# Identity of the self loops: from PSUM on ScalarE to SBUF on GpSimd, with another DRAM layout of two matrices

## The chip, the cores and the metric

The kernel runs on one NeuronCore of one Trainium2 chip. The time is the device time of one launch, in microseconds; the median of three runs of the kernel before is 2294.6 us (2289.54 to 2294.87). Engines are named as in the profile: PE is TensorE, PEld its weight load, DVE VectorE, ACT ScalarE, POOL GpSimd, SP the engine that issues most DMAs.

## The reference

A chain of four residual blocks over 3125 nodes with 256 features and 100000 edges. Edges come sorted by destination, and low destinations have many more edges than high ones (the square of a uniform number).

```python
dst = jnp.minimum((3125 * jax.random.uniform(..., (100000,)) ** 2.0).astype(jnp.int32), 49999)
...
def _spmm(src, dst, w, x, n):                       # used twice, with edge weights
    return jax.ops.segment_sum(w[:, None] * x[src], dst, num_segments=n)
for W, b, g, be in ((W1, b1, g1, be1), (W2, b2, g2, be2)):
    agg = _spmm(src, dst, edge_weight, x, n)
    h = (x + agg) @ W + b                           # the x here is the self loop
    x = jax.nn.gelu(_layer_norm(h, g, be), approximate=False)
...
def gcn_conv(x, edge_index, W, b, n_nodes):         # used twice, with counts
    loops = jnp.arange(n_nodes, dtype=edge_index.dtype)
    ...                                             # loops are joined to src and dst
    deg = jax.ops.segment_sum(jnp.ones_like(dst, dtype=x.dtype), dst, num_segments=n_nodes)
    dinv = jnp.where(deg > 0, jax.lax.rsqrt(deg), 0.0)
    ...
x = x + L0_gnn(layernorm(x)); x = x + L0_ffn(layernorm(x)[None])[0]
x = x + L1_gnn(layernorm(x)); x = x + L1_ffn(layernorm(x)[None])[0]
```

## The kernel before, in words

The sums over edges are done as dense products. The kernel first builds two matrices of 3200 x 3200 float32 (padded nodes): the weight matrix (the sum of edge weights between two nodes, plus the identity) and the count matrix (the number of edges, plus the identity). Both go to DRAM. Three passes then read them back in pieces and multiply them with the features.

**The build** takes the destinations in 400 windows of 8 nodes. Edges stand in chunks of 128; each meeting of a chunk with a window is a *pair*, 1200 with the padding at the end. Three engines work on pairs at once.

- DVE makes one-hot matrices for a batch of 8 pairs (six instructions, lines 993 to 998; 150 batches). Three batches may lie ahead of PE.
- PE adds each pair into PSUM with four bf16 matmuls (three at line 1353 for the weight's three parts, one at line 1354 for the counts). Two windows are a *group* and have two banks; the eight banks hold four groups. PE waits on `acc_free` before it writes into a group's banks, and each pair adds to `pair_done`.
- ACT takes a finished group (wait on `pair_done`): line 579 copies the two banks to `stage[half]` in SBUF, line 585 zeroes them, a drain follows, and line 553 (`self_loops`) writes the two windows' piece of the identity into both matrices' accumulators, which frees the banks (`acc_free`). PE then adds to it.

Ten groups (160 nodes) are a *unit*, and there are 20 units. `stage` has two halves, used in turn. At a unit's end ACT raises `unit_complete` right after the last copy, and copies the degree row (line 557, `degrees_of`, adds to `unit_summed`). SP waits for `unit_complete` and issues the two writes of the unit at line 474, 2 MB each, to the weight and to the count matrix. Before ACT fills a half again, `stage_free` waits until both writes of that half's last unit have landed and its degrees are taken; then ACT loads the unit's ten limits from a table (line 570). At the end ACT, PE and DVE meet in `compute_end`.

Eight matmuls at line 1330 write all banks once ahead of the build (`banks_opened`), and ACT waits for them.

**The passes** read a block of 320 columns (two units) in five DMAs of 800 KB (line 507; the first block at line 477) into `ring`, and PE multiplies (line 1417, `stream`), 1500 products of 128x128 by 320 float32 columns, with the layers' other work beside them. `ring` and `stage[0]` share memory, so the first block's DMAs wait until the second last unit is written.

There is a second way through the build for edges that are not sorted (`disordered > 0`); these inputs do not take it.

## Time and profile before

| | us |
|---|---|
| median of three runs | 2294.6 |
| the profiled run's own time | 2289.54 |
| its span in the trace | 2287.8 |
| build, first pair on PE to ACT's last copy of degrees | 107.6 to 692.8 |
| first product of the passes | 699.1 |

| engine | busy us | share of the span |
|---|---|---|
| PE | 2064.8 | 90% |
| DVE | 957.0 | 42% |
| ACT | 623.0 | 27% |
| POOL | 49.6 | 2% |

The shares are means over stages with different limits: in the passes PE is busy all the time, in the build it is not. The profile page says, for each group of instructions, how long it ran, and how long its engine was idle just before and what ended that. The granted clock of TensorE is given as a share of full speed (1.0 is 2.4 GHz, 0.5 is 1.2 GHz).

### The profile page before, as it was taken

To read this page: it belongs to the slowest core of one execution; us is meant where nothing else is said; L and a number is where in the kernel's file an instruction comes from. 1 tells how busy PE (TensorE), PEld (TensorE's weight loads), DVE (VectorE), ACT (ScalarE), POOL (GpSimd) and SP (SyncE) were. 2 spreads that over 40 slices of the span, in tenths; PEclk is the share of its full clock that TensorE was granted. 3 is DMA by queue.
4 is the path that set the end of the run, shared out by engine and by line. 5 is a ranking of instruction groups with operands and counts; after the bars stand their busy time and mean duration, and the time that the engine had idled before them with its cause. 6 is when DMAs were issued, how large, how long until landed. Compare 5 with 4: busy or idle time off the path is not lost.

```text
span 2287.8 us, 32669 instructions
## 1 busy us (share of the span) xinstructions
PE 2064.8 (90%) x11143; PEld 1596.8 (70%) x11144; DVE 957.0 (42%) x1977; ACT 623.0 (27%) x1057; POOL 49.6 (2%) x58
## 2 busy tenths in 40 slices
PE   1698888887678999999999979999999989999997
PEld 1388788777666777777777756657777767777776
DVE  5899999987760111111233332221332232222222
ACT  0014577787781200000111023320000012212121
POOL 2000000000000000000000000000000000000000
PEclk7799999998988999999999989989999999999999
DMA  2001333433457444444433310004334420000000
GB/s 77 1 0 72 143 143 143 197 161 161 198 213 216 127 136 140 142 143 137 125 115 126 115 58 1 0 0 144 115 117 127 128 89 1 12 12 0 11 11 10
DMA packets 70915, 221.13 MB, mean 97 GB/s; under 512 B 10300, under 2 KB 27354, under 8 KB 65754
## 3 DMA queue, kind: packets, MB, share of 16 engines
q1 hardware_dynamic: 56554, 213.41, 27.0%
q10 hardware_dynamic: 14320, 7.18, 1.3%
q8 instruction: 26, 0.43, 0.1%
q14 instruction: 15, 0.12, 0.0%
HBM read 135.45 MB, written 85.12 MB: 96 GB/s over the span
## 4 chain that ended last, share of the span: by engine, by line
issue 54%; PE 30%; DVE 8%; ACT 4%; ACTq 2%; DVEq 1%; DMA 0%; SPq 0%; POOL 0%; POOLq 0%
PE ps L1353 8%; PE ps L1434 8%; PE ps L1586 8%; DVE act_c L998 4%; PE ps L1354 3%; ACT ps L585 2%; ACT wide L579 2%; ACTq L570 1%; PE ps L1417 1%; PE ps L1325 1%; DVE act_c L993 1%; PE ps L1610 1%; DVE wide L1287 0%; DMA wide<-in_edge_weight_dram 0%; PE ps L1466 0%
## 5 line engine op out<-in xcount | busy, mean ns | idle before, releaser
L1353 PE MATMUL ps<-early,act_c 128*128 128x200 bf16 x3600 | 473.2, 261 | 105.4 <-ACT ps L553 47.7
L1417 PE MATMUL ps<-wide 128*128 128x320 f32 x2000 | 547.0, 434 | 0.0
L1417 PEld LDWEIGHTS ps<-wide 128*128 128x128 f32 x2000 | 379.3, 191 | 154.4 <-issue 1.7
L1353 PEld LDWEIGHTS ps<-early,act_c 128*128 128x128 bf16 x3600 | 343.0, 101 | 138.7 <-issue 131.4
L1354 PE MATMUL ps<-early,act_c 128*128 128x208 bf16 x1200 | 316.6, 264 | 0.0
L998 DVE TENSOR_TENSOR act_c<-act_c,pair_tab 128x1024 bf16<-128x1024 bf16 x450 | 282.9, 682 | 0.0
L1417 PE MATMUL ps<-wide,act_a 128*128 128x320 f32 x1000 | 274.7, 437 | 8.8 <-ACTq L618 8.8
L1417 PEld LDWEIGHTS ps<-wide,act_a 128*128 128x128 f32 x1000 | 192.1, 193 | 88.8 <-issue 11.8
L579 ACT COPY wide<-ps 128x816 f32<-128x816 f32 x200 | 167.2, 836 | 177.7 <-PE ps L1354 134.8
L1287 DVE SCALAR_TENSOR_TENSOR wide<-ps,small,wide 128x256 f32<-128x256 f32 x200 | 82.0, 477 | 266.6 <-PE ps L1434 266.4
L1095 DVE TENSOR_TENSOR wide<-ps,rows 128x1280 f32<-128x1280 f32 x10 | 14.9, 1492 | 419.4 <-PE ps L1434 419.4
L1586 PE MATMUL ps<-act_a,wide 128*128 (+1 forms) x640 | 188.9, 451 | 0.0
L1434 PE MATMUL ps<-early,act_c 128*128 128x256 f32 x800 | 181.8, 383 | 2.3 <-DVEq L1289 2.3
L1434 PEld LDWEIGHTS ps<-early,act_c 128*128 128x128 f32 x800 | 153.7, 192 | 28.0 <-issue 2.7
L585 ACT ACTIVATE ps<-ones 128x816 f32<-128x816 f32 x200 | 170.6, 853 | 8.1
L771 ACT ACTIVATE act_c<-ps,cols 128x320 f32<-128x320 f32 x160 | 84.4, 527 | 322.4 <-PE ps L1586 322.4
L1586 PEld LDWEIGHTS ps<-act_a,wide 128*128 128x128 f32 x640 | 125.5, 198 | 54.3 <-issue 11.0
L994 DVE TENSOR_TENSOR early<-rows 128x1600 bf16<-128x1600 bf16 x150 | 147.3, 982 | 0.0
L993 DVE TENSOR_TENSOR act_c<-rows,pair_tab 128x1024 bf16<-128x1024 bf16 x150 | 102.5, 684 | 70.3 <-PE ps L1354 68.8
L1354 PEld LDWEIGHTS ps<-early,act_c 128*128 128x128 bf16 x1200 | 121.3, 101 | 2.3
L692 ACT COPY wide<-ps 128x1280 f32<-128x1280 f32 x10 | 12.3, 1226 | 323.6 <-PE ps L1440 323.6
L717 ACT ACTIVATE act_c<-ps,cols 128x320 f32<-128x320 f32 x90 | 46.1, 524 | 101.4 <-PE ps L1508 99.3
(197 smaller groups left out, 1305.9 us busy)
## 6 DMA issues: line engine op xcount, KB each, us to landing
wide<-weight_matrix SPq DMA_DIRECT2D x100, 800.0 KB, 4.5
weight_matrix<-wide SPq DMA_DIRECT2D x20, 2000.0 KB, 6.2
count_matrix<-wide SPq DMA_DIRECT2D x20, 2000.0 KB, 10.8
wide<-count_matrix SPq DMA_DIRECT2D x50, 800.0 KB, 4.5
x_nodes<-in_x_dram ACTq DMA_DIRECT2D x1, 3072.0 KB
out_dram<-x_nodes SPq DMA_DIRECT2D x4, 640.0 KB
early<-in_L_ffn_w_dram SPq DMA_DIRECT2D x8, 256.0 KB, 5.4
wide<-in_L_ffn_w_dram SPq DMA_DIRECT2D x8, 256.0 KB, 4.2
```

The source lines that it names most:

```text
L579: act.copy(stage[half][:, :, k * GCOLS:(k + 1) * GCOLS].rearrange("p r (b j) -> p b r j", b=GROUP), group_ps.rearrange("p b (r j) -> p b r ...
L585: act.activation(group_ps, zero, ACT.Copy, scale=0.0)
L771: act.activation(moe_h[e % 2][:, m, half * SUB:(half + 1) * SUB], ps[:, m * 2 + half, 0:SUB], ACT.Gelu, bias=moe_b1[:, e, m:m + 1]).then_i ...
L993: dve.tensor_tensor(hot_lane[:, slot, 0], for_each(lane_wide, P), of_pairs(pair_tab[:, 0, first], P), ALU.is_equal).then_inc(lane_made, 1)
L994: dve.tensor_tensor(hot_key[:, slot, :, 0:WCOLS, :], for_each(key_wide, WCOLS), of_pairs(pair_key[:, first], WCOLS), ALU.is_equal)
L998: i = dve.tensor_tensor(hot_lane[:, slot, part], hot_lane[:, slot, 0], of_pairs(pair_tab[:, part, first], P), ALU.mult)
L1287: dve.scalar_tensor_tensor(moe_acc[:, t, :], tile_ps(4, t), gates_here[:, t, e:e + 1], moe_acc[:, t, :], ALU.mult, ALU.add).then_inc(dve_c ...
L1353: nc.tensor.matmul(weights, hot_lane[:, slot, part, two, :, k], hot_key[:, slot, two, 0:WCOLS, k], start=False, stop=True, skip_group_chec ...
L1354: nc.tensor.matmul(counts, hot_lane[:, slot, 0, two, :, k], hot_key[:, slot, two, :, k], start=False, stop=True, skip_group_check=True).th ...
L1417: i = nc.tensor.matmul(ps[:, 2 * sub + h, 0:SUB], features[:, q * QUADS + t, h * P:(h + 1) * P], ring[:, q, :, t, :], start=q == 0 and t = ...
L1434: i = nc.tensor.matmul(tile_ps(bank, t), src_t[:, h, t * P:(t + 1) * P], w[:, h, :], start=h == 0, stop=h == KD - 1)
L1586: i = nc.tensor.matmul(ps[:, m * 2 + half, 0:SUB], moe_w1[:, e, k, m * P:(m + 1) * P], act_a_t[:, k, nodes(s, half)], start=k == 0, stop=k ...
```

## The change

Four edits come together.

- ACT no longer writes the identity into PSUM. The drain and line 553 go, `acc_free` is raised by the zeroing instruction itself, and the eight opening matmuls and ACT's wait for them go too.
- POOL adds the identity in SBUF instead. For each unit it waits until ACT has zeroed all ten groups, does four in-place adds on `stage[half]` (two pieces of the unit for each of the two matrices, 320 columns in all), copies the degree row of 160 columns, waits for the five, and only then raises `unit_complete` and `unit_summed`.
- The matrices in DRAM lie in rows of 320 columns instead of 160. A write of half a block then goes out in 25 runs of 640 bytes for each partition, where it was one run of 16000. A read of the ring comes in runs of 6400 bytes, where it was 3200.
- The `ring` tile has the same order as the new rows, so PE reads 320 columns in one piece instead of two pieces of 160. The path for unsorted edges is changed as well.

```diff
-        weight_dram = nc.dram_tensor("weight_matrix", [2 * SUPERS, 2, P, TILES, UCOLS], F32).ap()
+        weight_dram = nc.dram_tensor("weight_matrix", [2 * SUPERS, P, TILES, SUB], F32).ap()
...
-        ring = wide[:, 0:8000].rearrange("p (a h b c) -> p a h b c", a=UNITS, h=2, b=QUADS)
+        ring = wide[:, 0:8000].rearrange("p (a b c) -> p a b c", a=UNITS, b=QUADS)
...
+                cols = slice(half * UCOLS, (half + 1) * UCOLS)
-                    sp.dma_start(matrix[ds(u2, 1), half, :, :, :].rearrange("a p t c -> (a p) t c"), stage[half][:, rows_of, :]).then_inc(written[half], 16)
+                    sp.dma_start(matrix[ds(u2, 1), :, :, cols].rearrange("a p t c -> (a p) t c"), stage[half][:, rows_of, :]).then_inc(written[half], 16)
...
-                            act.wait_ge(copies_done, s * (4 * UGROUPS) + group + 1)
-                            if k == UGROUPS - 1:
-                                act.sem_inc(unit_complete, 1)
-                            act.activation(group_ps, zero, ACT.Copy, scale=0.0)
-                            act.drain()
-                            self_loops(first_bank, group + SETS, s).then_inc(acc_free, 1)
-                        degrees_of(u4, half, s).then_inc(unit_summed, 1)
+                            act.wait_ge(copies_done, u2 * (2 * UGROUPS) + half * UGROUPS + k + 1)
+                            act.activation(group_ps, zero, ACT.Copy, scale=0.0).then_inc(acc_free, 1)
...
+            with pool.Fori(0, SUPERS) as s:
+                enter(s, 4 + 16)
+                for step in range(4):
+                    half = step % 2
+                    pool.wait_ge(acc_free, SETS + UGROUPS * (s * 4 + step + 1))
+                    d0 = step * UCOLS
+                    while d0 < (step + 1) * UCOLS:
+                        d1 = min((step + 1) * UCOLS, (d0 // P + 1) * P)
+                        cols = slice(d0 - step * UCOLS, d1 - step * UCOLS)
+                        eye = ident[:, d0 % P:d0 % P + d1 - d0]
+                        for kind in range(2):
+                            part = stage[half][:, ds(s * SUPER + kind * TILES + d0 // P, 1), cols].rearrange("p a c -> p (a c)")
+                            pool.tensor_tensor(part, part, eye, ALU.add).then_inc(pool_chain, 1)
+                        d0 = d1
+                    pool.tensor_copy(degree_part[:, ds(s * SCOLS + step * UCOLS, UCOLS)], stage[half][:, 2 * TILES, :]).then_inc(pool_chain, 1)
+                    pool.wait_ge(pool_chain, count(5))
+                    pool.sem_inc(unit_complete, 1)
+                    pool.sem_inc(unit_summed, 1)
+            leave(SUPERS)
...
-            for bank in range(ACCS):
-                i = nc.tensor.matmul(ps[:, bank, 0:PCOLS], ones_half[:, :], ones_half[:, 0:1].broadcast_to([P, PCOLS]), start=True, stop=True)
-            i.then_inc(banks_opened, 1)
...
-                        i = nc.tensor.matmul(ps[:, 2 * sub + h, 0:SUB], features[:, q * QUADS + t, h * P:(h + 1) * P], ring[:, q, :, t, :],
+                        i = nc.tensor.matmul(ps[:, 2 * sub + h, 0:SUB], features[:, q * QUADS + t, h * P:(h + 1) * P], ring[:, q, t, :],
```

ACT, the last two groups of a unit and the start of the next, before (`wide` is `stage`, `ps` the accumulators, `dinv_row` holds the degree row, `early` the table of limits):

```order
L579 COPY wide<-ps 128x2x51x8 [waits pair_done]
L582 REGISTER_ALU
L585 ACTIVATE ps<-ones 128x2x408 [waits copies_done]
L553 ACTIVATE ps<-ident 128x2x2x8
L557 ISA
L557 COPY dinv_row<-wide 128x160
L543 REGISTER_ALU [waits counts_written_1,weights_written_1]
L570 ISA [waits unit_summed]
L570 TENSOR_LOAD early
L579 COPY wide<-ps 128x2x51x8 [waits pair_done]
```

The same place after:

```order
L561 COPY wide<-ps 128x2x51x8 [waits pair_done]
L564 REGISTER_ALU
L565 ACTIVATE ps<-ones 128x2x408 [waits copies_done]
L543 REGISTER_ALU [waits counts_written_1,weights_written_1]
L553 ISA [waits unit_summed]
L553 TENSOR_LOAD early
L561 COPY wide<-ps 128x2x51x8 [waits pair_done]
```

Two of ACT's instructions for the identity and the degrees are gone; the two waits at the unit's start stand where they stood.

POOL, the first unit of the loop, after (in the kernel before nothing stands between its two 25 column instructions, lines 839 and 843):

```order
L822 ISA [waits acc_free]
L822 TENSOR_TENSOR wide<-wide,ident 128x128
L822 ISA
L822 TENSOR_TENSOR wide<-wide,ident 128x128
L822 ISA
L822 TENSOR_TENSOR wide<-wide,ident 128x32
L822 ISA
L822 TENSOR_TENSOR wide<-wide,ident 128x32
L824 ISA
L824 COPY dinv_row<-wide 128x160
L825 ISA
L814 ISA [waits pool_chain]
```

These five instructions now stand between ACT's last zeroing and the unit's writes.

SP, the writes of a unit and the first block's reads, as a piece of the difference:

```order
-L474 DMA weight_matrix<-wide 128x4000
-L474 DMA count_matrix<-wide 128x4000
-L477 DMA wide<-weight_matrix 128x2x800 x5
+L474 DMA weight_matrix<-wide 3200x1x160
+L474 DMA count_matrix<-wide 3200x1x160
+L477 DMA wide<-weight_matrix 128x1600 x5
```

No DMA changes its place; the writes go from 128 runs each to 3200, the reads from 256 to 128.

## Rows read from the trace of the kernel before

**Rows 1.** Windows view: stretch; PE, PEld, DVE, ACT, POOL busy (instructions); clock, DMA share, GB/s.

```profile
107.00:325.90 218.90, 193.62 (x2008) 182.63 (x2009) 212.03 (x374) 96.06 (x160) 0.00 (x0) 0.96 0.18 76
325.90:427.50 101.60, 86.97 (x873) 82.00 (x872) 93.01 (x164) 75.18 (x126) 0.00 (x0) 0.92 0.38 161
427.50:664.80 237.30, 183.92 (x1764) 167.30 (x1762) 192.23 (x336) 185.53 (x311) 0.00 (x0) 0.91 0.41 173
```

**Rows 2.** The same view of line 1354 alone (one instruction a pair).

```profile
427.50:664.80 237.30, 118.21 (x441) 45.30 (x441) 0.91 0.41 173
```

**Rows 3.** Timeline of ACT: start, us, instruction, [idle before it <- what ended it].

```profile
568.13 0.83 ACT L579 COPY wide<-ps 128x816 f32<-128x816 f32 x1
...
573.86 0.84 ACT L579 COPY wide<-ps 128x816 f32<-128x816 f32 x1 [3.33 <-issue]
574.73 0.85 ACT L585 ACTIVATE ps<-ones 128x816 f32<-128x816 f32 x1
575.73 0.20 ACT L553 ACTIVATE ps<-ident 128x32 f32 x1
575.86 0.83 ACT L579 COPY wide<-ps 128x816 f32<-128x816 f32 x1
...
593.68 0.31 ACT L557 COPY dinv_row<-wide 128x160 f32 x1
```

**Rows 4.** Timeline of PE, the build's first pair and the first after a stall.

```profile
107.56 0.68 PE L1353 MATMUL ps<-early,act_c 128*128 128x200 bf16 x3 [5.86 <-ACT ps L553]
...
576.15 0.44 PE L1353 MATMUL ps<-early,act_c 128*128 128x200 bf16 x3 [3.69 <-ACT ps L553]
```

**Rows 5.** Timeline of ACT and DVE at the build's start.

```profile
103.89 3.16 ACT L562 ACTIVATE ps<-ones 128x816 f32<-128x816 f32 x4
...
113.09 0.69 DVE L993 TENSOR_TENSOR act_c<-rows,pair_tab 128x1024 bf16<-128x1024 bf16 x1 [2.62 <-PE ps L1354]
```

**Rows 6.** Timeline of ACT in the last unit.

```profile
679.39 0.85 ACT L585 ACTIVATE ps<-ones 128x816 f32<-128x816 f32 x1
...
690.36 0.84 ACT L579 COPY wide<-ps 128x816 f32<-128x816 f32 x1 [3.79 <-PE ps L1354]
```

**Rows 7.** Timeline of SP, then DMA from 568 to 592: us to landing; packets, MB, share.

```profile
569.60 0.38 SPq L474 DMA_DIRECT2D count_matrix<-wide  x1
...
count_matrix<-wide SPq DMA_DIRECT2D x1, 2000.0 KB, 10.8
...
q1 hardware_dynamic: 288, 4.10, 40.1%
```

**Rows 8.** Queue rows: 512 byte loads, 0 to 30; 1024 byte stores, 1966 to 1975.

```profile
q1 hardware_dynamic: 2436, 1.20, 14.9%
...
q1 hardware_dynamic: 656, 0.66, 21.2%
```

**Rows 9.** POOL by shape: busy us, mean ns, idle before and its releaser.

```profile
L843 POOL TENSOR_TENSOR small<-small 128x25 f32<-128x25 f32 x1 | 4.3, 4319 | 658.2 <-ACT small L641 658.2
...
L807 POOL TENSOR_SCALAR_AFFINE_SELECT ident<-ident 128x128 f32<-128x128 f32 x1 | 0.3, 294 | 0.2 <-POOL ident L805 0.2
```

**Rows 10.** The page's costliest groups, DVE's longest and most frequent one-hot instructions.

```profile
L998 DVE TENSOR_TENSOR act_c<-act_c,pair_tab 128x1024 bf16<-128x1024 bf16 x450 | 282.9, 682 | 0.0
...
L994 DVE TENSOR_TENSOR early<-rows 128x1600 bf16<-128x1600 bf16 x150 | 147.3, 982 | 0.0
```

**Rows 11.** Timeline from the build's end into the first pass; a DMA row of the page.

```profile
674.78 2.88 SPq L477 DMA_DIRECT2D wide<-weight_matrix  x5
...
699.14 29.12 PE L1417 MATMUL ps<-wide,act_a 128*128 128x320 f32 x100 [8.82 <-ACTq L618]
...
wide<-weight_matrix SPq DMA_DIRECT2D x100, 800.0 KB, 4.5
```

**Rows 12.** Timeline of weight loads: a ring product, and one with whole rows of 320.

```profile
1119.94 21.30 PEld L1417 LDWEIGHTS ps<-wide 128*128 128x128 f32 x80
...
2093.19 4.17 PEld L1586 LDWEIGHTS ps<-act_a,wide 128*128 128x128 f32 x16
```

More of the change, by code:

```diff
@@ L329, in build_program @@
         window_free = sem("window_free")
-        banks_opened = sem("banks_opened")
         ahead_ready = sem("ahead_ready")
@@ L588, in _ @@
[L588 removed]
+                            act.wait_ge(copies_done, u2 * (2 * UGROUPS) + half * UGROUPS + k + 1)
+                            act.activation(group_ps, zero, ACT.Copy, scale=0.0).then_inc(acc_free, 1)
             with act.If(disordered > 0):
+                act.sem_inc(acc_free, SETS)
+                act.sem_inc(window_free, 2)
                 act.wait_ge(tables_ready, 1)
[L592 to L607 removed]
@@ L609, in _ @@
+                with act.Fori(0, BUNITS // 2) as u2:
+                    for half in range(2):
+                        stage_free(u2, half)
+                        with act.Fori(0, UGROUPS) as k:
+                            for par in range(GROUP):
+                                w = u2 * 2 * UWINS + half * UWINS + k * GROUP + par
+                                end = act.value_load(base_tab[:, ds(w + 1, 1)], min_val=2, max_val=10 ** 6)
                                 act.wait_ge(onehot_used, end + OH)
-                                cols = slice((k * GROUP + par) * WIN, (k * GROUP + par + 1) * WIN)
+                                cols = ds(k * GCOLS + par * WIN, WIN)
@@ L616, in _ @@
+                            act.drain().then_inc(acc_free, 1)
             compute_end(act, 1)
@@ L1357, in _, with pair @@
             pe.sem_inc(onehot_used, OH)
-            def pair(g, par):
+            def pair(g, par, first):
                 slot = pe.snap(g % OH)
```

61 lines of the change are left out of this document (14 added, 47 removed).

## The prediction, before the changed kernel was run

> **What bounds the kernel now.** I read the busy tenths first: the passes (from 699 on) have PE full, the build (107 to 692) has no engine full. All edits but the ring's layout touch the build, so I asked for the busy times by stretch [rows 1]. Up to 325.9 DVE is busy 212.0 of 218.9 us: it bounds. From 325.9 to 427.5 it is busy 93.0 of 101.6. From 427.5 to 664.8, ten units, it is busy 192.2 of 237.3 only, PE 183.9, and ACT 185.5, and still a unit takes 23.7 us for its 44 pairs [rows 2]. The timeline of ACT says why [rows 3]: it goes from group to group without a gap. A group is copy at 573.86, zeroing at 574.73, identity at 575.73, next copy at 575.86, so 2.00 us here, and all ten take 19.8 (573.86 to 593.68); the degrees take 0.31, and then ACT stands 3.33 us before the next copy, which is the load of the unit's limits, not a wait for anybody. 19.8 + 0.3 + 3.4, and some tenths more every fourth unit, is 23.6: ACT's own program is the bound there. PE and DVE wait for it: PE stands 3.69 us before line 1353 for the release of banks [rows 4].
>
> **The change, part by part.** The sum is made against the profiled execution, 2289.5 us (span 2287.8); the median is 5.1 above it.
>
> *1. ACT's group.* The drain and the identity go. Copy to zeroing is 0.87 with a wait for the copy between them; four zeroings in a row take 3.16, 0.79 each [rows 5]. So copy to copy becomes 0.87 + 0.86 = 1.73, where it was 1.98 (19.8 / 10). A unit is then 17.3 + 3.4 + 0.3 (some tenths at each turn of the loop, which now comes every second unit) = 21.0 instead of 23.6. What is late next is DVE: 192.2 / 10 = 19.2 a unit on the mean, about 21 to 22 in the first two units of the stretch and 17 to 19 at its end. I add 0.4 for the coupling, since three engines with buffers of three batches and four groups are never exactly at the slowest one's rate. 21.4 x 10 = 214, so **-23** (bounds -27 with no coupling, and what part 3 says above).
>
> *2. The other stretches.* 325.9 to 427.5: DVE idles 8.6 us of four units, of which ACT's faster groups can give back a part, and POOL may take a part away (part 4): -1 (bounds -8 and +5). Last unit: the copy of the last group (690.36) waits for PE's padding pairs, 10.1 us after the zeroing of the sixth group has ended at 680.24 [rows 6]; PE can begin the last group only when the sixth has given its banks back, so that tail stays near 9.9, while the load and six groups ahead of it get 6 x 0.25 shorter, and the degrees (0.31) and the last identity (0.2) go: -2. Start: PE's first pair waited 5.86 us for ACT [rows 4], DVE then stood 2.62 us with three batches made [rows 5]. Without the eight matmuls and ACT's four identities PE can start when the first batch is made, about 3.8 us earlier, which covers DVE's gap: -2.6 (bounds 0 and -3.8).
>
> *3. The unit's writes.* The end of the last copy to the landing of the counts took 11.4 us (568.97 to 569.60 + 10.8 [rows 3, 7]). Of this the data are 0.401 x 24 us = 9.6 us for 288 packets, mostly of 16000 bytes. After, there are 6400 packets of 640 bytes. No row shows a store of that size. Near it stand loads of 512 bytes, 0.149 x 16 x 30 us / 2436 = 29.4 ns each, and stores of 1024 bytes, 0.212 x 16 x 9 / 656 = 46.5 ns [rows 8]. Between them by size, 33.7 ns; x 6400 / 16 engines = 13.5 us. So landing comes 11.4 - 9.6 + 13.5 = 15.3 us after the signal, bounds 11.4 (no dearer than now) and 20.4 (46.5 ns each).
>
> This decides with POOL's part. A half is refilled two units later, and what must fit is: load and ten groups of unit u (20.7), POOL t, landing L, against two units of ACT, 42.0. So t + L up to 21.3 costs nothing; from there on a unit is (20.7 + t + L) / 2; and at 26.7 the unit is 23.7 as now. Behind the wait for the half stands all of ACT's work, then PE's banks, then DVE: this wait holds everybody.
>
> *4. POOL.* Four adds on 320 columns together and a copy of 160. The trace has no add. The selection on 128x128, which reads and writes one tile, takes 0.294, and the tensor_tensor with a power 4.32 us for 25 columns [rows 9]. I take the first for each of the five: 1.5 us, because the power is another computation than the add; by the power's rate the five would be some 80 us and the kernel over 2700, an end that I keep only as a reason for the far side. Each POOL instruction may also have to wait for one of DVE's of 0.68 to 0.98 us [rows 10], which would be up to 5 more; I take t = 3 (1 to 7). t + L = 18.3, under 21.3: hidden. Both upper bounds together, 27.4, are just beyond break-even.
>
> What POOL does may also hold DVE, where DVE bounds: nothing up to its own 1.5 us a unit. I take 1.0 for the five units before 325.9: **+5** (0 to +8).
>
> No row shows POOL and DVE working at once. The Trainium skill (SBUF — State Buffer, "Who interferes with whom") says that a DVE instruction with two SBUF inputs and a GpSimd instruction that reads SBUF exclude each other for a whole instruction, and all of DVE's one-hot instructions have two. By that rule the hold would be the full 1.5 us in each DVE bound unit, and the sum would be some 4 us worse. The same skill (GPSIMD Engine Reference, "Elementwise — side-by-side cycle accounting") gives 4497 ns for an add of 2048 columns, from which I estimate 0.7 us for the 320; no run here shows that yet.
>
> *5. After the build.* The last writes are issued about 4 us later and take 4 longer, but they are awaited only for the second block's reads and for the degrees at line 1466, and PE has 29.1 us of products before that [rows 11]. The first block's reads, now issued 16 us before the build ends, would be issued about 0 to 2 us before it; five reads of 800 KB took 4.5 us each to landing [rows 11], and PE starts 6.3 us after the build's end: hidden, 0 (up to +3). POOL is not among the three engines that meet at the end.
>
> *6. The ring's layout.* 80 weight loads of the ring's products take 21.30 us, 266 ns each; 16 of a product whose operand already lies in whole rows of 320 take 4.17, 261 ns [rows 12]. PE streams pieces of 160 as fast as 320: 0 (0 to -1). The reads are hidden as they are.
>
> Sum: -23 - 1 - 2 - 2.6 + 5 + 0 = **-24**. From 2289.5 this is 2265.5; on the median's scale 2294.6 - 24 = **2271**.
>
> **The rivals.**
>
> *A, the forecast*: 2271 on the median's scale, own range 2256 to 2281.
>
> *B, a new bound takes a part.* Either t + L comes out at 24, so a unit is 22.4 and part 1 gives 13 instead of 23; or PE does: its busy time is 18.4 a unit (183.9 / 10, part of it at half clock, the granted clock being 0.91 over the stretch [rows 1]), and with a stall of 4 in each unit, as the one of 3.69 [rows 4], it needs 22.4 as well. For it: PE was stalled in each unit. Against: the stall is ACT's load, and PE has room of four groups. -24 + 10 = -14: 2281.
>
> *C, the writes and POOL take over: slower.* Place: `stage_free` on ACT. It decides from t + L = 26.7. If stores of 640 bytes cost 55 ns (more than the 46.5 of 1024 bytes), L is 23.8, and with t = 8 (five waits behind DVE and dearer adds) the sum is 31.8 and a unit 26.3: ten units +26, the four before (25.4) +4, the DVE bound +5, start -2.6, last unit 0: +32, 2327. For it: neither price has a row, two prices at their upper bounds suffice, and nothing in the loop has slack beyond 2 units. Against: the nearest rows on each side lie well below.
>
> *D, it doesn't do what it says.* ACT's copy to copy stays near 2 us, because the copy after a zeroing waits for PE or for the queue, or POOL holds DVE all along (14 units x 1.5, and more in waits): gains and losses cancel, 2294.
>
> **How the numbers follow.** A 0.48, B 0.22, C 0.20, D 0.10. The bound of 0.3% (7 us) is about what a measurement of this kernel tells from no change. Faster: nearly all of A, four fifths of B, a fifth of D: 0.67. Same: 0.12. Slower: C and a little of D: 0.21. The likeliest is A, 2271. The range reaches down to A with parts 1 and 2 at their ends (-27 - 8 - 2 - 3.8 = -41, 2254) and up over B and D into the near part of C: 2254 to 2308.
>
> **What would show it.** Right: ACT's copies 1.73 apart in the late build, units of 21 to 22 us there, and the gap before a unit's first copy still 3.3 to 3.9. Landing of the counts 14 to 17 us after issue, POOL's five in 1.5 to 5 us. Wrong: a gap before the first copy of 6 us or more that a DMA ends (C, or B), DVE instructions longer than 0.68 and 0.98 or more DVE busy time than 212 before the fifth unit's end (D), the first product waiting for a ring read (part 5), and weight loads of line 1417 (now renumbered) off 266 ns (part 6). The forecast as a whole fails if a 640 byte store takes over 50 ns or POOL's five over 8 us.

## The result, and the profile after

| | before | after |
|---|---|---|
| median, us | 2292.4 (4 runs, 2289.5 to 2294.9) | 2348.2 (4 runs, 2342.5 to 2361.1) |
| ratio after/before | | 1.0252, 95% interval 1.0207 to 1.0297 |
| the profiled run's own time | 2289.5 | 2370.1 |
| its span | 2287.8 | 2367.8 |

The profiled run of the changed kernel stands beside its four runs and is slower than any of them. One run of e9 below, 2319.2 us, is over 1.5% above that kernel's fastest and is left out of its figures.

The forecast was 2271, faster, with a range up to 2308. The kernel became 2.5% slower.

The first thing to ask of the two traces is where the 80.6 us between the profiled runs lie. ACT's first copy of each unit is a good milestone, since everything in the build passes through it. The last column ("again") is a second profiled run of the changed kernel.

| milestone, us | before | after | again |
|---|---|---|---|
| first copy of unit 3 | 237.9 | 268.5 | 266.4 |
| unit 6 | 329.5 | 376.3 | 352.4 |
| unit 10 | 431.2 | 484.2 | 460.5 |
| unit 20 | 668.5 | 744.0 | 720.8 |
| first product of the passes | 699.1 | 776.8 | 753.6 |
| own time | 2289.5 | 2370.1 | 2351.7 |

Of +80.6, 53.0 are there at unit 10, another 22.5 come in the ten late units (259.8 us where it was 237.4 and 214 were forecast), 2.1 up to the first product and 3.0 later. "Again" has +29.3, +23.0, +2.2 and +7.7. So both the stretch where DVE bounds and the late one got slower. The passes, from the first product to the end, take 1590.4, 1593.3 and 1598.1 us; over all the profiled runs below they take 1584.3 to 1603.2, whatever the edit, so a difference of a few us in one time says nothing of the build.

The windows view of after, against [rows 1] (stretch; PE, PEld, DVE, ACT, POOL busy and instructions; clock, DMA share, GB/s):

```profile
107.00:325.90 218.90, 172.97 (x1805) 162.03 (x1804) 191.48 (x338) 67.53 (x80) 93.07 (x11) 0.92 0.13 38
325.90:427.50 101.60, 62.97 (x614) 58.26 (x612) 68.89 (x118) 47.82 (x57) 34.65 (x20) 0.82 0.54 161
427.50:664.80 237.30, 175.87 (x1736) 162.38 (x1733) 192.00 (x326) 151.64 (x184) 124.25 (x47) 0.88 0.49 146
```

DVE, which bounded the first stretch with 212, is busy 191 there; ACT is busy 151.6 instead of 185.5 in the third and yet it is not done sooner; and POOL, forecast at 3 us a unit, is busy 124 us in the third, which here holds some nine units. The lines view of POOL by shape (busy us, mean ns | idle before and its releaser) names the operation:

```profile
L822 POOL TENSOR_TENSOR wide<-wide,ident 128x128 f32 x20 | 99.7, 5002 | 216.9 <-ACT ps L565 216.9
L822 POOL TENSOR_TENSOR wide<-wide,ident 128x64 f32 x20 | 72.2, 3631 | 139.0 <-ACT ps L565 139.0
...
L824 POOL COPY dinv_row<-wide 128x160 f32 x20 | 29.4, 1472 | 0.0
```

An add of 128 columns was taken at 0.294 us [rows 9]; its mean is 5.0. The mean hides two kinds, which the timeline of POOL shows (start, us, instruction; "x4" holds the four adds of a unit; in brackets the idle time before):

```profile
191.75 57.56 POOL L822 TENSOR_TENSOR wide<-wide,ident 128x128 f32 x4 [112.16 <-ACT ps L565]
249.25 0.32 POOL L824 COPY dinv_row<-wide 128x160 f32 x1
250.01 1.28 POOL L822 TENSOR_TENSOR wide<-wide,ident 128x96 f32 x4 [0.44 <-POOL dinv_row L824]
...
292.19 42.64 POOL L822 TENSOR_TENSOR wide<-wide,ident 128x64 f32 x4 [40.64 <-ACT ps L565]
...
588.41 14.47 POOL L822 TENSOR_TENSOR wide<-wide,ident 128x128 f32 x4 [22.59 <-ACT ps L565]
602.83 3.62 POOL L824 COPY dinv_row<-wide 128x160 f32 x1
606.89 9.14 POOL L822 TENSOR_TENSOR wide<-wide,ident 128x96 f32 x4 [0.44 <-POOL dinv_row L824]
```

Four adds of 320 columns together take 1.28 us and the copy 0.32 when DVE stands (250.01). Beside a busy DVE each POOL instruction takes about 3.6 us, the add and the copy alike, whatever its width. And twice the first one took far longer: 57.56 and 42.64 us for the four, 56.7 and 41.7 of them for the first add alone. DVE (timeline; the last instructions before it stands still, twice, and two batches of the late stretch):

```profile
246.27 1.89 DVE L986 TENSOR_TENSOR act_c<-act_c,pair_tab 128x1024 bf16<-128x1024 bf16 x3
...
331.81 1.89 DVE L986 TENSOR_TENSOR act_c<-act_c,pair_tab 128x1024 bf16<-128x1024 bf16 x3
...
537.05 0.98 DVE L982 TENSOR_TENSOR early<-rows 128x1600 bf16<-128x1600 bf16 x1
537.96 0.34 DVE L983 TENSOR_TENSOR early<-rows 128x64 bf16<-128x64 bf16 x1
538.23 1.88 DVE L986 TENSOR_TENSOR act_c<-act_c,pair_tab 128x1024 bf16<-128x1024 bf16 x3
540.03 0.68 DVE L981 TENSOR_TENSOR act_c<-rows,pair_tab 128x1024 bf16<-128x1024 bf16 x1
540.63 0.98 DVE L982 TENSOR_TENSOR early<-rows 128x1600 bf16<-128x1600 bf16 x1
541.54 0.34 DVE L983 TENSOR_TENSOR early<-rows 128x64 bf16<-128x64 bf16 x1
```

The two long adds end when DVE has stopped: at 248.5 (191.75 + 56.73), DVE at 248.2 (246.27 + 1.89), and at 333.9 (292.19 + 41.68), DVE at 333.7 (331.81 + 1.89). In the late stretch a batch takes 3.58 us (541.54 - 537.96). The small instruction of 64 columns takes 0.27 to 0.48 there where it takes 0.18 when POOL rests, and the POOL instructions end inside it (the adds that begin at 588.41 end at 602.88; the small instruction runs from 602.66 to 602.93): that is the place, once a batch, where one POOL instruction gets in. DVE loses 0.1 to 0.3 us by it, POOL waits a whole batch.

What this does to the others stands in the chain of work that ended last (start, us, what) between two units' first copies:

```profile
567.44 3.31 ACTq L553
570.79 0.85 ACT wide L561
...
588.44 0.14 POOL wide L822
...
592.12 10.76 POOL wide L822 x3
602.88 3.58 POOL dinv_row L824
606.67 0.55 SPq L474
607.32 13.41 DMA count_matrix<-wide
620.97 3.66 ACTq L553
624.67 0.85 ACT wide L561
```

ACT fills a half of `stage`, POOL takes 18.0 us over it (588.44 to 606.46), SP and the DMA 14.5, ACT's load 3.7, and only then is the half filled again: 53.9 us for two units (570.79 to 624.67). Before, one long gap of ACT was 3.33 [rows 3]. Now (timeline of ACT):

```profile
268.48 0.84 ACT L561 COPY wide<-ps 128x816 f32<-128x816 f32 x1 [37.42 <-issue]
...
624.67 0.84 ACT L561 COPY wide<-ps 128x816 f32<-128x816 f32 x1 [19.35 <-issue]
625.54 0.85 ACT L565 ACTIVATE ps<-ones 128x816 f32<-128x816 f32 x1
626.33 0.83 ACT L561 COPY wide<-ps 128x816 f32<-128x816 f32 x1
627.19 0.85 ACT L565 ACTIVATE ps<-ones 128x816 f32<-128x816 f32 x1
627.98 0.83 ACT L561 COPY wide<-ps 128x816 f32<-128x816 f32 x1
```

A group of ACT is 1.65 us (627.98 - 626.33), as wanted; the 19.35 us before every second unit eat it. "Issue" names no releaser, because the wait is for a semaphore that the DMA raises and the load of the limits is behind it; the chain shows what it was.

PE at the build's start and behind it, with the weight loads of a ring product, and the page's DMA rows (against [rows 4, 7, 11, 12]; before, the counts landed 10.8 after issue and PE waited 8.82 for its first product):

```profile
104.95 0.68 PE L1338 MATMUL ps<-early,act_c 128*128 128x200 bf16 x3 [12.50 <-ACT ps L549]
...
776.76 28.71 PE L1402 MATMUL ps<-wide,act_a 128*128 128x320 f32 x100 [13.01 <-DMA wide<-weight_matrix]
...
813.63 18.27 PE L1402 MATMUL ps<-wide,act_a 128*128 128x320 f32 x60 [2.49 <-DMA wide<-weight_matrix]
...
1208.22 21.30 PEld L1402 LDWEIGHTS ps<-wide 128*128 128x128 f32 x80
```

```profile
weight_matrix<-wide SPq DMA_DIRECT2D x20, 2000.0 KB, 8.0
count_matrix<-wide SPq DMA_DIRECT2D x20, 2000.0 KB, 13.8
```

The build starts 2.6 us earlier (104.95). The weight loads take the same 21.30. The counts land 13.8 us after issue. The first product waits for a ring read and comes 13.0 us after ACT's last copy has begun (763.78), where it was 8.8 (690.36 to 699.14).

### The profile page after: what moved, and what is told of

The parts are those of the page before. It is cut to its first block, busy times and chain, and to the rows that moved or that the text cites. A ratio compares the mean times of both kernels' runs of the same rounds, so it can differ in the third digit from the quotient of the medians.

```text
span 2367.8 us, 32365 instructions
## 1 busy us (share of the span) xinstructions
PE 2045.9 (86%) x11132; PEld 1586.3 (67%) x11136; DVE 966.1 (41%) x1977; ACT 579.5 (24%) x833; POOL 347.7 (15%) x158
## 4 chain that ended last, share of the span: by engine, by line
issue 58%; PE 23%; DVE 5%; DMA 5%; POOL 4%; ACT 3%; ACTq 1%; SPq 0%; DVEq 0%; POOLq 0%
PE ps L1571 7%; PE ps L1419 7%; DMA count_matrix<-wide 5%; PE ps L1338 4%; POOL wide L822 3%; ACT wide L561 2%; DVE act_c L986 2%; PE ps L1339 1%; ACTq L553 1%; PE ps L1313 1%; ACT ps L565 1%; POOL dinv_row L824 1%; PE ps L1595 1%; DVE act_c L981 1%; DVE wide L1275 0%
## 5 line engine op out<-in xcount | busy, mean ns | idle before, releaser
L1338 PE MATMUL ps<-early,act_c 128*128 128x200 bf16 x3600 | 466.8, 259 | 194.7 <-ACT ps L565 129.9
L1338 PEld LDWEIGHTS ps<-early,act_c 128*128 128x128 bf16 x3600 | 339.2, 100 | 226.3 <-issue 219.7
L822 POOL TENSOR_TENSOR wide<-wide,ident 128x128 f32 (+3 forms) x80 | 269.7, 3401 | 389.5 <-ACT ps L565 388.2
L836 POOL TENSOR_TENSOR small<-small 128x5 f32<-128x5 f32 x25 | 29.2, 1168 | 1099.3 <-DVE small L1071 1099.3
L1419 PEld LDWEIGHTS ps<-early,act_c 128*128 128x128 f32 x800 | 153.8, 193 | 28.1 <-issue 2.7
L739 ACT ACTIVATE act_c<-ps,cols 128x320 f32<-128x320 f32 x160 | 84.4, 527 | 322.6 <-PE ps L1571 322.6
L1339 PEld LDWEIGHTS ps<-early,act_c 128*128 128x128 bf16 x1200 | 120.3, 100 | 1.9
## 6 DMA issues: line engine op xcount, KB each, us to landing
count_matrix<-wide SPq DMA_DIRECT2D x20, 2000.0 KB, 13.8
```

The source lines that it names most:

```text
L739: act.activation(moe_h[e % 2][:, m, half * SUB:(half + 1) * SUB], ps[:, m * 2 + half, 0:SUB], ACT.Gelu, bias=moe_b1[:, e, m:m + 1]).then_i ...
L822: pool.tensor_tensor(part, part, eye, ALU.add).then_inc(pool_chain, 1)
L1338: nc.tensor.matmul(weights, hot_lane[:, slot, part, two, :, k], hot_key[:, slot, two, 0:WCOLS, k], start=False, stop=True, skip_group_chec ...
L1339: nc.tensor.matmul(counts, hot_lane[:, slot, 0, two, :, k], hot_key[:, slot, two, :, k], start=False, stop=True, skip_group_check=True).th ...
L1419: i = nc.tensor.matmul(tile_ps(bank, t), src_t[:, h, t * P:(t + 1) * P], w[:, h, :], start=h == 0, stop=h == KD - 1)
```

## The experiments

Ratios are to the kernel before, run on the same chip, with 95% intervals. The theory: POOL's instructions, which read SBUF, get in beside DVE once a batch or not at all; that time stands in the loop half of `stage` -> POOL -> writes -> ACT. The rivals: it is the new DRAM layout (dearer writes), or ACT's own program, or any work of POOL.

**e1, the layout alone** on the kernel before.

> The kernel before with the new DRAM and ring layout alone; identity and degrees stay on ACT. Theory 1 (GpSimd's reads of SBUF are shut out by VectorE's one-hot instructions, and that alone makes the change slow): the counts land 13 to 14 us after issue instead of 10.8, which still fits into the 20 us that ACT needs for the other half, so the time is that of before, 2292, within 5 us (a few us more if the first product now waits for its first reads). Rival 1 (the 640 byte writes make it slow): 2310 to 2350, with ACT idle before a unit's first copy 6 us or more, ended by a DMA.

```diff
-        weight_dram = nc.dram_tensor("weight_matrix", [2 * SUPERS, 2, P, TILES, UCOLS], F32).ap()
+        weight_dram = nc.dram_tensor("weight_matrix", [2 * SUPERS, P, TILES, SUB], F32).ap()
```

Measured: 2293.7, ratio 1.0009 (0.9994 to 1.0024), and the counts land 13.8 us after issue. The layout makes each pair of writes 3 us longer and costs nothing measurable in this kernel, whose loop has slack.

**e2, all but the layout.**

> The changed kernel with the old layout (writes of 16000 byte runs, reads of 3200), so GpSimd's adds stay and the writes land in 10.8 us. Theory 1: each GpSimd instruction still takes 2.5 to 3.6 us beside a busy VectorE, and the first ones some 40 to 57 us; only about 3 us of 14 go from the chain of each pair of units, so 2315 to 2345, clearly slower than 2292. Rival 1: 2265 to 2275, since the writes are as fast as before.

```diff
-        weight_dram = nc.dram_tensor("weight_matrix", [2 * SUPERS, P, TILES, SUB], F32).ap()
+        weight_dram = nc.dram_tensor("weight_matrix", [2 * SUPERS, 2, P, TILES, UCOLS], F32).ap()
```

Measured: 2308.3, ratio 1.0062 (1.0040 to 1.0085). Slower even with the cheap writes (10.7 us). The four adds of a unit take 11.6 to 15.7 us where DVE is busy, and the copy 3.62:

```profile
189.65 14.37 POOL L821 TENSOR_TENSOR wide<-wide,ident 128x128 f32 x4 [111.41 <-ACT ps L564]
203.97 3.62 POOL L823 COPY dinv_row<-wide 128x160 f32 x1
```

The median add is 3.5 us and the longest 4.9; no long exclusion is in this profile. The 40 us between e2 and the changed kernel are thus not the layout's own (e1), but the layout's together with POOL's time, and the long exclusions. The milestones divide them. "Again" is later than e2's profiled run by 21.3 us at unit 6 (352.4 against 331.1), the long exclusion at unit 2; 0.4 more come to unit 10, 9.6 in the ten late units (260.3 against 250.7) and 9.7 up to the first product, which in e2 does not wait for a ring read (2.1 us after ACT's last copy has begun). The passes give 5.1 back: 36.0 in all (2351.7 - 2315.7).

**e3, POOL without its five instructions.** The identity is left out of both matrices, ACT takes the degrees, POOL only passes the signal on.

> The changed kernel without the identity (it is left out of both matrices); the degree row is copied by ACT after the last zeroing, and GpSimd only waits and raises unit_complete. The new layout stays. Theory 1: with t near 0 the write chain is hidden again and ACT's shorter group shows: copies 1.65 to 1.75 us apart, units of 21 to 22 us late in the build, 2292 - 24 = 2268 (2258 to 2278). Rival 1: still 2320 or more. Rival 2 (ACT's shorter group brings nothing, since PE or VectorE become the bound): 2285 to 2295.

```diff
-                            pool.tensor_tensor(part, part, eye, ALU.add).then_inc(pool_chain, 1)
...
-                    pool.tensor_copy(degree_part[:, ds(s * SCOLS + step * UCOLS, UCOLS)], stage[half][:, 2 * TILES, :]).then_inc(pool_chain, 1)
```

Measured: 2263.5, ratio 0.9877 (0.9852 to 0.9903), so -27 us. From unit 10's first copy to unit 20's it takes 218.8 us, 21.9 a unit, where I had forecast 21.4. But it isn't ACT's own program that takes 21.9 here. The load of the limits (source views of its line: ns minimum, median, maximum), before and in e3, and ACT in e3:

```profile
L570 ACTq TENSOR_LOAD <-early x20: 1027/3420/3522, 107.6 to 665.0; - x20
```

```profile
L553 ACTq TENSOR_LOAD <-early x20: 978/987/1012, 101.4 to 642.0; - x20
```

```profile
557.33 0.31 ACT L566 COPY dinv_row<-wide 128x160 f32 x1
557.89 0.84 ACT L561 COPY wide<-ps 128x816 f32<-128x816 f32 x1 [0.26 <-PE ps L1337]
...
569.40 0.84 ACT L561 COPY wide<-ps 128x816 f32<-128x816 f32 x1 [3.17 <-PE ps L1337]
```

The load took 3.4 us in the kernel before and takes 1.0 here, and it is over before the unit's first copy: the gap there is 0.26 to 0.65 us in the late units, where it was 3.33. ACT waits for PE instead, 48.0 us in all between 427.5 and 664.8. Why the load became short is not shown; in the changed kernel it is long again only where ACT has waited for its half. The five instructions cost 85 us (2348.2 - 2263.5), although where DVE stands still they take 1.6 us a unit.

**e4, five memsets in their place**, of the same sizes, which write SBUF and read none of it (they overwrite parts of the matrices).

> As e3_no_adds, but GpSimd does five memsets of the same sizes on the same stage half before it raises unit_complete (their output spoils the matrices; the identity is left out). They write SBUF and read nothing. Theory 1 in the form that only GpSimd's reads collide with VectorE's second SBUF operand: memsets of 0.1 to 0.3 us each, the time of e3_no_adds within 5 us. Rival 3 (any GpSimd instruction is shut out beside a busy VectorE): memsets of 2.5 us and more, and 2315 to 2350.

```diff
-                            pool.tensor_tensor(part, part, eye, ALU.add).then_inc(pool_chain, 1)
+                            pool.memset(part, 1.0).then_inc(pool_chain, 1)
```

Measured: 2258.7, ratio 0.9854 (0.9837 to 0.9871), like e3. Beside the busy DVE they take what a free POOL needs:

```profile
L828 POOL MEMSET wide<- 128x160 f32 x20 | 4.6, 232 | 0.0
...
L826 POOL MEMSET wide<- 128x128 f32 x20 | 3.5, 205 | 203.1 <-ACT ps L566 203.1
```

It is the POOL instructions that read SBUF that wait, not POOL's work as such.

**e5, two adds instead of four** (each on both matrices), and the copy, in the new layout.

> The changed kernel, but each GpSimd add takes both matrices' rows at once: 2 adds of twice the columns and the degree copy, 3 instructions a unit for 5; same columns, same result, new layout. Theory 1a (beside a busy VectorE a GpSimd instruction gets in once in a one-hot batch, 3.6 us, whatever its size): t = 3 x 3.6 = 11 us for 18, t + L = 26.4, a unit of (20.7 + 26.4) / 2 = 23.6 as before the change, so 2290 to 2302. Rival 4 (the price goes by columns): t stays 18, 2335 to 2350.

```diff
-                            pool.tensor_tensor(part, part, eye, ALU.add).then_inc(pool_chain, 1)
+                        pool.tensor_tensor(part, part, eye.unsqueeze(1).broadcast_to([P, 2, d1 - d0]), ALU.add).then_inc(pool_chain, 1)
```

Measured: 2298.9, ratio 1.0023 (1.0013 to 1.0033). The same elements in fewer instructions gain 49 us: the price is by instruction, and not by column. The profile has again one long exclusion at unit 2, from 190.49 to 247.8; but the profiled run took 2320.6 and the other ten 2295.0 to 2300.4, and whether these had the exclusion too is not shown.

**e6, two adds, the old layout, degrees by ACT.** It does all that the reference asks.

> As e5_two_adds, with the layout of before and the degree row copied by ACT after its last zeroing, so two GpSimd instructions a unit. Theory 1a: t = 7.3, L = 11.4, sum 18.7, under the 21.3 that ACT's two units leave; hidden, and ACT's shorter group shows: the 2263 of e3_no_adds plus the holds of VectorE, 2 x 0.23 us in nine units, so 2262 to 2275, faster than before by 0.9 to 1.3%. Rival 4: t still 14, t + L = 26, 2288 to 2300.

```diff
+                        act.copy(degree_part[:, ds(u2 * (2 * UCOLS) + half * UCOLS, UCOLS)], stage[half][:, 2 * TILES, :]).then_inc(unit_summed, 1)
...
-                    pool.wait_ge(pool_chain, count(5))
+                    pool.wait_ge(pool_chain, count(2))
```

Measured: 2252.9, ratio 0.9835 (0.9815 to 0.9856), the fastest of all. A unit takes 20.9 us in the late stretch. It shows what the change's first part is worth when POOL and the writes stay hidden. ACT waits for PE here too, 47.5 us between 427.5 and 664.8, and all its loads of limits take 0.98 to 1.02 us.

**e7, a gap in DVE's stream**: the changed kernel with a drain of DVE behind the instruction of 64 columns.

> The changed kernel with a drain of VectorE in each of the 150 batches, after the 64 column piece. Theory 1b (GpSimd gets in only where VectorE's instructions leave a gap): the drain's gap is a second way in, GpSimd's instructions fall from 3.6 to about 2 us, none takes over 10 us, and t is 10 for 18; VectorE pays 0.1 to 0.2 us a batch in the stretch that it bounds. So 2295 to 2330, faster than the 2348 of the changed kernel. Rival 5 (a gap doesn't matter, the turn comes by something else): instructions of 3.6 us and more as before, 2350 to 2375 with VectorE's price on top.

```diff
                         dve.tensor_tensor(hot_key[:, slot, :, WCOLS:KCOLS, :], for_each(dst_wide, WIN), of_pairs(pair_dst[:, first], WIN), ALU.is_equal)
+                        dve.drain()
```

Measured: 2302.0, ratio 1.0044 (1.0030 to 1.0058): 46 us faster than the changed kernel, though the gap costs DVE 38.1 us in all (0.25 in each of 150 batches):

```profile
L987 DVE TENSOR_TENSOR act_c<-act_c,pair_tab 128x1024 bf16<-128x1024 bf16 x450 | 287.9, 695 | 38.1 <-issue 38.1
```

```profile
L822 POOL TENSOR_TENSOR wide<-wide,ident 128x128 f32 x20 | 14.6, 747 | 207.4 <-ACT ps L565 207.4
...
L824 POOL COPY dinv_row<-wide 128x160 f32 x20 | 11.2, 562 | 0.0
```

An add of 128 columns goes from 5.0 to 0.75 us, and no exclusion is left. Four adds take 2.0 to 3.3 us beside a busy DVE, so the gap of a batch lets more than one through. Against e3, which has the same layout, no adds and no gaps, it is 38.5 us slower, about what the gaps cost.

**e8, one load of the limits for two units**, on the kernel before, as a test of the reading that ACT's own program was the bound in the late build.

> The kernel before with one load of the limits for two units (20 values) instead of one for each (10), nothing else. This tests the reading that ACT's program (20.1 us of groups and 3.4 us of load) is what bounds ten units late in the build: if it is, about 3.4 us go in every second unit, 5 x 3.4 = 17 less than 2292, 2272 to 2282. If PE or VectorE bound there, the same time within 4 us. If 20 values take twice as long to load as 10, the same time too, and the gap before the first copy of every second unit is 6 us or more.

```diff
-                            end_tab[:, ds(s * (4 * ENDS) + u4 * ENDS, UGROUPS)], engines=(mybir.EngineType.Activation,), min_val=1, max_val=PPAD + SLOTS * BATCH,
+                                end_tab[:, ds(s * (4 * ENDS) + u4 * ENDS, 2 * UGROUPS)], engines=(mybir.EngineType.Activation,), min_val=1, max_val=PPAD + SLOTS * BATCH,
```

Measured: 2279.4, ratio 0.9943 (0.9924 to 0.9962). Every second gap of ACT went, the other grew from 3.33 to 4.29:

```profile
550.04 0.84 ACT L581 COPY wide<-ps 128x816 f32<-128x816 f32 x1 [4.29 <-issue]
...
570.95 0.83 ACT L581 COPY wide<-ps 128x816 f32<-128x816 f32 x1
```

That is (2 x 3.33 - 4.29) / 2 = 1.2 us a unit of ACT's program, but the ten late units got only 2.8 us shorter together (234.6 against 237.3), since ACT now waits for PE: 24.4 us in all between 427.5 and 664.8, where it was 8.2. Of the 9.5 us between the two profiled runs 3.4 are there at the first product (695.7 against 699.1) and 6.1 lie in the passes, which the edit doesn't touch. The time fell into the expected range, but the profile doesn't bear out the reason: ACT's program was at most a little longer than what PE and DVE need, and not the bound by 1.2 us a unit.

**e10, e6 in the new layout.**

> The changed kernel with the new layout, but with two adds for a unit (each on both matrices at once) and the degrees taken by ScalarE: the fifth study's kernel without GpSimd's copy of the degrees, and e6 with the new layout. It tests the formula for a unit, (20.7 + t + L) / 2. From e6, t is 5 to 8 us (two instructions, one each in a batch of VectorE's); from the new layout L is 14.5 to 15.5 with the counts landing 13.8 us after issue. Theory (the formula holds, GpSimd's time and the landing add up in one loop): t + L is 20 to 23, so a unit is 21 to 22 us: 0 to 10 us above e6, 2253 to 2263, and ScalarE's gap before a unit's first copy is 3.3 to 4.5 us. Rival (the new layout costs nothing by itself, as e1 shows, so it costs nothing here): 2251 to 2255. Second rival (what the profiles of the changed kernel and of e5 show, GpSimd shut out for 40 to 57 us at some units in the first 300 us, comes with the new layout in whatever form): such a stretch shows in this profile too, and the time is 2265 to 2285.

```diff
-        weight_dram = nc.dram_tensor("weight_matrix", [2 * SUPERS, 2, P, TILES, UCOLS], F32).ap()
+        weight_dram = nc.dram_tensor("weight_matrix", [2 * SUPERS, P, TILES, SUB], F32).ap()
```

Measured: 2309.7, ratio 1.0076 (1.0040 to 1.0113). All three expectations were too low. The late unit is 22.2 us, within the first theory. Most of the rest is at the start: one exclusion of 57.3 us at unit 2 (190.99 to 248.2) leaves unit 6 at 354.3 where it is 323.1 in e6. Of the 59.9 us between the two profiled runs 31.2 are there, 4.8 come up to unit 10, 12.2 in the ten late units, 1.0 up to the first product and 10.7 in the passes, in which PE waits 5.1 us for a ring read in its second group of products.

**e9, e6 with e8's single load.**

> e6 (two adds on both matrices at once, old layout, degrees by ScalarE) and, as in e8, one load of limits for two units. If ScalarE's own program still bounds the late build in e6, each second unit saves some 3 us less a longer load, 1.2 us a unit as e8 did over the kernel before: 10 units, 2240 to 2246. If in e6 VectorE bounds the late build already (it was busy 205 of 237 us there), or the wait for the half does, it brings 0 to 5: 2248 to 2253.

```diff
-                            end_tab[:, ds(u2 * (2 * ENDS) + half * ENDS, UGROUPS)], engines=(mybir.EngineType.Activation,), min_val=1, max_val=PPAD + SLOTS * BATCH,
+                                end_tab[:, ds(u2 * (2 * ENDS), 2 * UGROUPS)], engines=(mybir.EngineType.Activation,), min_val=1, max_val=PPAD + SLOTS * BATCH,
```

Measured: 2282.1 (2275.2 to 2300.3), ratio 0.9963 (0.9938 to 0.9989), where 2240 to 2253 was expected: a miss. The single load had nothing to save, because in e6 the load no longer stands between two units: the late unit is 21.5 us here and 20.9 in e6. And its profile has the exclusion too, in the old layout:

```profile
192.03 57.21 POOL L825 TENSOR_TENSOR wide<-wide,ident 128x256 f32 x2 [112.27 <-ACT ps L566]
```

Unit 6's first copy comes at 350.0, 26.9 later than in e6, of 33.6 us between the two profiled runs.

**e11, the changed kernel once more**, one profile.

> The changed kernel once more, for one more profile. In its first profile GpSimd's first add of the second unit took 56.7 us and one of a later unit 42 us, and that run was 20 us above the median of the others. If these stretches are a matter of how the loops happen to lie in time, this profile has them at other places, shorter or not at all, and the run's time moves with their sum: 2335 to 2350 without one of over 20 us, 2360 to 2375 with two. If they are fixed by the program (the data of those units), they stand at the same units with the same length, and the time is 2365 to 2375.

Measured: 2351.7. At unit 2 the same stretch of 57.55 us (from 189.66), at unit 4 13.09 instead of 42.64. So the first stands in both profiles of this program, the second does not; the run is 18.4 us shorter than the first profiled one, and unit 6 comes 23.9 us earlier.

**e12, a gap in one of three batches**, on e9.

> e9 with VectorE's drain (the gap of e7, 0.25 us) in every third batch. Theory (e9's profile has one stretch of 57.2 us in which GpSimd does not get in, that is what separates its 2283 from the 2243 expected, and a single gap in VectorE's stream ends such a stretch): no GpSimd instruction takes over 3 x 3.41 + 0.25 = 10.5 us, no 57 us stretch; the gaps cost 50 x 0.25 = 12.5 us, some 8 of it where VectorE bounds; the time is 2246 to 2262. Rival (the 57 us are not what makes e9 slow, or a gap in one of three batches does not let GpSimd in): 2285 to 2295, with an instruction of over 11 us in the profile.

```diff
+                        if n % 3 == 0:
+                            dve.drain()
```

Measured: 2258.3, ratio 0.9855 (0.9832 to 0.9877), 24 us below e9 although DVE has 50 gaps more:

```profile
194.00 4.43 POOL L825 TENSOR_TENSOR wide<-wide,ident 128x256 f32 x2 [114.77 <-ACT ps L566]
235.58 5.91 POOL L825 TENSOR_TENSOR wide<-wide,ident 128x192 f32 x2 [37.15 <-ACT ps L566]
```

The exclusion is gone, and with it e9's loss. No kernel of these is faster than e6. e12's interval overlaps e6's, and in its profile no POOL add takes over 4.4 us; why e6 has no exclusion is not known.

## Why the prediction was wrong, by its own steps

**Part 1, ACT's group: right; ACT's unit: wrong, and hidden by luck.** It is 1.65 us from copy to copy when nothing blocks, where 1.73 was forecast; the forecast took 0.86 for a zeroing, and its own row gave 0.79, so 1.66. But the unit of 21.0 was added up with a load of 3.4 us between units, and "the gap before a unit's first copy still 3.3 to 3.9" was a sign of being right. In e3 that gap is 0.26 to 0.65, the load takes 1.0, and ACT waits for PE. The 21.9 us a unit of e3, near the forecast's 21.4, come from PE and DVE and not from the sum that gave them. Nor does e8 show that ACT's program bounded the ten late units before.

**Part 2: the start right**, 2.6 us. The last unit and the middle stretch were overrun by part 4. How parts 1 and 2 come out alone shows in e3: its profiled run is 28.1 us shorter than the one before, where -23 - 1 - 2 - 2.6 = -29 stood, but 7.0 of this are there at unit 10 (forecast 3.6), 18.5 in the ten late units (forecast 23), 6.0 from unit 20 to the first product (forecast 2), and the passes are 3.4 longer. The sum is right because the parts' errors cancel.

**Part 3, the writes: right in size, and the formula too where the half is waited for.** L was forecast at 15.3 from the signal; it is 14.5 (606.46 to 620.97), the counts landing in 13.8. With t = 18.0 the formula gives (20.7 + 18.0 + 14.5) / 2 = 26.6 a unit; the chain shows 53.9 / 2 = 26.9. Over the ten late units the mean is 26.0. ACT waits for one of the two halves only, and there POOL takes 14.8 to 18.1 us, 16.2 on the mean, so the formula gives 25.7; over the other half POOL takes 9.1 to 11.0 and ACT hardly waits (0.4). The table has the mean over both halves (t is POOL's busy time from unit 10's to unit 20's first copy, divided by ten, and the unit that stretch's tenth; the time is the median of all runs, the rest the profiled run's):

| kernel | t | counts landing | late unit | time |
|---|---|---|---|---|
| after | 13.0 | 13.8 | 26.0 | 2348.2 |
| e2 | 13.2 | 10.7 | 25.1 | 2308.3 |
| e5 | 6.2 | 13.9 | 23.2 | 2298.9 |
| e10 | 4.1 | 13.9 | 22.2 | 2309.7 |
| e7 | 3.1 | 13.9 | 22.3 | 2302.0 |
| e6 | 4.9 | 10.8 | 20.9 | 2252.9 |
| e3 | 0.0 | 13.9 | 21.9 | 2263.5 |

The unit falls with t + landing from the changed kernel to e10. Below that it doesn't: e6 has more than e3 and the shorter unit, and in both of them ACT waits for PE and not for its half. e7's unit also holds its gaps. The time doesn't follow the late unit alone, since the exclusions of the start are in it too.

**Part 4, t = 3 with bounds 1 to 7: the step that failed.** "Each POOL instruction may also have to wait for one of DVE's of 0.68 to 0.98 us, which would be up to 5 more." It measures 3.6 us an instruction, 14.8 to 18.1 us in the late units that ACT waits for, and in some units 42 to 57 for a single one. The price of the add alone was right (1.28 for four, 0.32 for the copy; 1.5 for the five was forecast). What was wrong is the picture of the waiting: DVE's instructions stand back to back, and in these traces POOL does not get in at the end of just any of them, but at the short one of 64 columns (0.27 to 0.48 us for 0.18), or in a gap. Why it gets in there is not shown. My upper bound was put together from the length of one DVE instruction; the nearest thing in the trace of before that could have given it is the length of the batch, 3.41 us, times five instructions = 17, and with L = 15.3 that is past the point of 26.7 that I had worked out myself.

I cited the Trainium skill (SBUF — State Buffer, "Who interferes with whom") at that place: a DVE instruction with two SBUF inputs shuts out a GpSimd instruction that reads SBUF for its whole length, but not one that only writes. The runs bear out both halves (e4's memsets take 125 to 232 ns, e2's adds beside a busy DVE 3.6 us), and the copy, with one input, waits like the add (up to 3.62 in e5, 0.56 on the mean in e7). I priced the rule at 4 us of hold on DVE and not at POOL's wait, which stands in the loop. The same section says that the engine which starts first holds the other off; in these runs DVE held off POOL over many instructions of its own, one behind another, and lost 0.1 to 0.3 us for each instruction of POOL's.

**The hold on DVE: 5 us (0 to 8) was too much.** Over the whole span DVE is busy 957.0 us before, 966.1 after, 956.4 in e3 and in e4, so POOL's 100 instructions cost it some 9. But up to unit 6, where DVE bounds, its short instructions take 184 ns on the mean in the changed kernel, 196 in "again" and 231 in e2, where they took 179: over 62 batches that is 0.3, 1.1 and 3.2 us. POOL was shut out there, or found DVE standing still.

**The early stretch had no term.** POOL's first instruction at unit 2 waits until DVE stops (248.2). DVE stops, since ACT waits for the half from 231.1 (268.48 - 37.42), PE for the banks, and then DVE's three batches are full. e9 and e6 put its price at 27 us (350.0 - 323.1), "again" and e2 at 21; in the two profiles of the changed kernel unit 6 is 46.8 and 22.9 us later than before, the first with the second exclusion at unit 4 as well.

**Part 5: wrong.** "0 (up to +3)": the first product comes 13.0 us after ACT's last copy has begun, where it came 8.8 after, so 4.2 later; and without the wait for a ring read it would come earlier than before, 2.1 to 2.3 after in e2, e3 and e6, so the wait costs some 11. The first block's reads are issued only at 772.37, after the build's end, because POOL's t delays the write that they wait for. In e3, with t = 0, the first product doesn't wait for them.

**Part 6, the ring's layout: right.** 80 weight loads take 21.30 us in both.

**The rivals.** What happened has rival C's place (`stage_free` on ACT), its formula and its point of decision. C had 0.20, and its price was put on the store (L = 23.8) with t = 8; it was the other way round, L = 14.5 and t = 18. Its +26 for the ten late units is near the 22.5 measured, but from two prices that were both wrong. Even so its 2327 falls short by 21, for want of the exclusions at the start. B and D don't fit: PE is busy less than before, and ACT's groups did become shorter.

**What stays open.** Why POOL's first instruction at unit 2 gets in after a batch in e2 and e6, and not at all in the changed kernel, e5, e9 and e10. DVE runs the same instructions in all, and POOL's request comes 0.2 to 0.3 us after the small instruction's start in each of them (189.65 after 189.46 in e2, 192.03 after 191.77 in e9), so neither the layout nor the place in the batch, as far as the times tell it, sets them apart. e12 shows that one gap in three batches ends it, not what starts it. Each kernel but the changed one has one profile, so how often its other runs have an exclusion is not known. Open is also why the load of the limits takes 1.0 us where it took 3.4.

## What to carry to other kernels

Before work is moved to GpSimd beside a VectorE that runs instructions with two SBUF inputs without a gap, price each GpSimd instruction that reads SBUF at VectorE's whole loop period, not at one instruction, and ask whether the result stands in a loop of buffers; if it does, few wide instructions, a write-only form, or a 0.25 us gap in VectorE's stream were worth 24 to 90 us here (e12 against e9, e4 against the changed kernel). A bound for a cost without a row should be taken from the longest thing that the waiting could span. A sum that comes out right is no proof of its terms: ask the trace for the gap that each term names. And two edits that look small alone (the layout +0.1%, the rest of the change in the old layout +0.6%) can cost far more together (+2.5%): here some 19 of 36 us, in the late units and at the first product, where both prices lie on one path; the exclusion at the start, which comes with either layout (e9), gives another 21, and the passes 5 back.

## What the runs showed that I had not expected

- POOL's instructions beside DVE's back-to-back two-input instructions: 3.6 us each whatever the width, against 0.3 us alone (1.28 for four adds, 0.32 for the copy); up to 57 us for one, ended by DVE's stop.
- Memsets of the same sizes beside the same DVE: 125 to 232 ns.
- With a gap of 0.25 us in each batch of 3.75 us the adds took 0.56 to 0.75 us on the mean; with one gap in three batches there was no long exclusion.
- A DMA of 2 MB in 3200 runs holds SP's queue 3.9 to 12.2 us (median 4.1) when another stands ahead of it (count matrix, line 474), where the same DMA took 0.38 before [rows 7], and the pair lands in 13.8 us instead of 10.8.
- The load of a unit's ten limits took 3.4 us on the median before, and 1.0 in e3 and e6, where it began before ACT's last zeroing of the unit had ended (556.9 against 557.4 in e3).
